# Five chained stages: shared buffers for each next stage's first loads, normalisation moved into channel attention's last pass, loops written out

## The reference

```python
x = context_xattn(x, ctx, w_q, w_k, w_v, w_o, alpha)   # 16 context rows per batch, x + alpha * delta
x = channel_xattn(x, ctx, ...)   # heads over the 256-row axis (16 heads of 64), attention between the 512 features
    # q, k, v = W @ z + Winj @ u;  x = W_o @ attention + b_o + z
    # m, var over the rows (axis 1);  (x - m) * rsqrt(var + 1e-5)
x = token_xattn(x, ctx, ...)     # layernorm, masked self attention, + x;  layernorm, cross attention, + x
    #                              then layernorm, gelu(x @ w1 + b1) @ w2 + b2, + x   (w1 512x2048, w2 2048x512)
x = recurrent(x, ...)            # layernorm, mixes, a scan over the tokens, group norm, gated feed forward
```

## Time and profile before

| | us |
|---|---|
| median of 3 runs | 3933.54 (3931.42 to 3935.23) |
| the profiled execution | 3925.65 |
| its span | 3923.7 |
| PE busy | 3475.4 (89%) |
| DVE busy | 2354.8 (60%) |
| POOL busy | 1995.9 (51%) |
| ACT busy | 1816.2 (46%) |
| PE weight loads | 2678.3 (68%) |
| mean granted clock of PE | 0.955 |

### The profile page before, as it was taken

The page is one execution under the profiler, slowest core; times in us unless marked ns, Lnnn a source line. Parts: engine busy times, 40 slices in busy tenths (PEclk is TensorE's granted clock), DMA queues, the critical chain, the costliest instruction groups (busy, mean ns, idle before and its releaser), DMA issues. The chain is left out here.

```text
span 3923.7 us, 61889 instructions
## 1 busy us (share of the span) xinstructions
PE 3475.4 (89%) x23616; PEld 2678.3 (68%) x23616; DVE 2354.8 (60%) x2915; ACT 1816.2 (46%) x4207; POOL 1995.9 (51%) x1018
## 2 busy tenths in 40 slices
PE   8979999999999999589989994999867888888876
PEld 5868778768877877277877783888745555555543
DVE  2445655565565555367778775555438677766771
ACT  1134554565465455366667664444422332333311
POOL 1135665565566556345556662455525555555562
PEclk9989999999999999799999997999989999999988
DMA  3231211111111111211021113000030000000000
GB/s 131 73 143 44 77 55 59 62 67 66 55 67 65 45 45 43 93 35 37 28 76 50 39 39 110 17 20 21 19 134 12 1 17 17 17 18 1 12 11 16
DMA packets 108138, 189.84 MB, mean 48 GB/s; under 512 B 13409, under 2 KB 32097, under 8 KB 106721
## 3 DMA queue, kind: packets, MB, share of 16 engines
q1 hardware_dynamic: 105696, 181.97, 13.5%
q10 hardware_dynamic: 2176, 4.19, 0.3%
HBM read 160.97 MB, written 25.17 MB: 47 GB/s over the span
## 5 line engine op out<-in xcount | busy, mean ns | idle before, releaser
L825 POOL TENSOR_TENSOR l_pr<-l_pr,l_inv 128x1024 f32<-128x1024 f32 x256 | 479.5, 1894 | 370.6 <-DVE l_inv L885 370.6
L734 ACT ACTIVATE l_pr<-l_ps_s,l_top 128x512 f32<-128x512 f32 x512 | 347.2, 691 | 335.2 <-DVE l_top L881 280.0
L1255 POOL TENSOR_TENSOR tok_pr<-tok_pr,tok_ma 128x1024 f32<-128x1024 f32 x128 | 305.3, 2408 | 281.5 <-DVE tok_pr L1620 281.5
L2374 POOL TENSOR_TENSOR rec_rs<-rec_sE,rec_rT 128x1024 f32<-128x1024 f32 x128 | 321.9, 2516 | 241.8 <-DVE rec_sE L2761 235.9
L820 POOL TENSOR_TENSOR l_x_lo<-l_zu,l_x_hi 128x2048 fp32r<-128x2048 f32 x63 | 288.5, 4580 | 238.6 <-ACT l_x_hi L718 238.6
L881 DVE TENSOR_REDUCE l_top<-l_ps_s 128x2 f32<-128x1024 f32 x256 | 301.3, 1219 | 11.9 <-PE l_ps_s L582 11.9
L2761 DVE TENSOR_TENSOR_SCAN rec_sE<-rec_wE,rec_ps_v 128x1024 f32<-128x1024 f32 x128 | 292.7, 2287 | 4.9
L592 PE MATMUL l_ps_t<-l_ident,l_pr 128*128 128x128 f32 x2048 | 275.4, 278 | 5.8 <-POOL l_pr L825 3.1
L592 PEld LDWEIGHTS l_ps_t<-l_ident,l_pr 128*128 128x128 f32 x2048 | 223.6, 141 | 79.2 <-issue 63.5
L1501 ACT ACTIVATE tok_pr<-tok_pr,tok_shift 128x256 f32<-128x256 f32 x512 | 253.5, 498 | 12.6 <-DVE tok_shift L1628 11.8
L739 ACT ACTIVATE l_pT<-l_ps_t 128x512 f32<-128x512 f32 x256 | 153.5, 600 | 82.6 <-PE l_ps_t L592 82.6
(11 more groups left out here) (374 smaller groups left out, 10182.6 us busy)
## 6 DMA issues: line engine op xcount, KB each, us to landing
l_zu<-x SPq DMA_DIRECT2D x64, 512.0 KB, 3.7
l_zu<-in_c SPq DMA_DIRECT2D x64, 512.0 KB, 4.6
l_w_raw<-in_L_w_qk SPq DMA_DIRECT2D x16, 512.0 KB, 6.8
tok_xs<-x SPq DMA_DIRECT2D x16, 512.0 KB, 3.9
x<-tok_xb SPq DMA_DIRECT2D x16, 512.0 KB, 2.8
l_xt<-in_xT SPq DMA_DIRECT2D x8, 512.0 KB, 6.2
l_ct<-in_cT SPq DMA_DIRECT2D x8, 512.0 KB, 7.2
l_xn<-in_x SPq DMA_DIRECT2D x8, 512.0 KB, 4.8
```

What stands on the lines that cost most here:

```text
L734: act.activation(pr[t][:, h, :], ps_s[:, t % 2, h, :], ACT.Exp, bias=top[:, t, h:h + 1], accum_out=mass[:, t, h:h + 1]).then_inc(exped, 1)
L825: pool.tensor_tensor(pr[t][:, :, :], pr[t][:, :, :], inv[:, t, :].unsqueeze(2).to_broadcast([P, 2, FEAT]), ALU.mult).then_inc(scaled, 1)
L1255: pool.tensor_tensor(tile, tile, ma[u][:, :, :].rearrange("p t k -> p (t k)").unsqueeze(1).to_broadcast([P, 2, TT * TOK]), ALU.add).then_i ...
L2374: pool.tensor_tensor(rs[j % 2][:, :, :], sE[j % 2][:, :, :], rT[s][:, :, :], ALU.mult).then_inc(rs_made, 1)
```

## The change

Three buffers belong to the whole program now (`Ahead`: two of 128x4x512, one of 128x2x512). The SP stream of a stage loads into them, near its own end, what the next stage reads first, with semaphores of the next stage that the `clear` between the two keeps: for channel attention the Q and K weights of the first pass and the first batch's rows, for the token attentions the Q and K weights and the first batch's rows, for the MLP the first two column pieces of w1 and the first batch's rows. The next stage reads them there, and its own first loads are gone; its further loads move up.

Channel attention's normalisation is done per batch during units 8 to 15 of the last pass: after a batch's last `add` VectorE sums the two row tiles (`sum_tokens`), in the next unit PE makes the mean with one matmul ahead of `mix`, VectorE centres ahead of `split_output`, ScalarE squares after `round_output`, POOL sums the two tiles of squares at the unit's end, and in the unit after that PE makes the variance with one matmul and VectorE copies it to SBUF. Logarithms and roots of batches 0 to 4 are taken in the last unit, those of 5 to 7 at the end. The stores are issued in another order.

The MLP's other twelve half pieces (128x2x512) are loaded into a ring of three buffers and rounded and split inside the first batch, two to a chunk for six chunks; b1 and b2 are loaded behind the first three halves. The `Fori` loops of token attentions, MLP and recurrent block become written-out bodies; the loop of context attention stays.

```diff
+class Ahead:
+    def __init__(self, nc, ctx):
+        self.pieces = [ctx.enter_context(nc.sbuf_tensor(f"ahead_piece{i}", [P, FT, FEAT], F32)) for i in range(2)]
+        self.rows = ctx.enter_context(nc.sbuf_tensor("ahead_rows", [P, TT, FEAT], F32))
+class AheadSignals:
+    def __init__(self, semaphores, block):
+        self.piece_loaded = [semaphores.allocate(f"{block}_piece_loaded{i}") for i in range(2)]
+        self.rows_loaded = semaphores.allocate(f"{block}_rows_loaded")
+        self.all = self.piece_loaded + [self.rows_loaded]
...
+            for src, a in enumerate((x1, c)):
+                sp.dma_start(ahead.pieces[1][:, 2 * src:2 * src + 2, :], a[0, :, :].rearrange("(t p) n -> p t n", p=P)).then_inc(following.rows_loaded, 16)
+            for part in range(2):
+                sp.dma_start(ahead.pieces[0][:, 2 * part:2 * part + 2, :].rearrange("p s n -> p (s n)"), w_after[0, :, part, :]).then_inc(
+                    following.piece_loaded[part], 16)
             for u in range(2):
...
+            return g == COUPLES and b > BATCH
+        EARLY = BATCH - 3
...
-            load_zu(1, 0)
-            load_w(0, 0)
...
+            sp.dma_start(ahead.pieces[0][:, :, :], w_after[0].rearrange("(t p) n -> p t n", p=P)).then_inc(following.piece_loaded[0], 16)
+            sp.wait_ge(x_split, of(COUPLES, UNITS - 1, 1, 0))
+            sp.dma_start(ahead.pieces[1][:, :, :], w_after[1].rearrange("(t p) n -> p t n", p=P)).then_inc(following.piece_loaded[1], 16)
...
+            store(3, 1, 2, stored)
+            store(1, 0, 2, stored)
+            store(4, 1, 3, stored)
+            sp.wait_ge(first_stored, 16)
...
+                        pe.wait_ge(*((var_kept, b - BATCH - 2) if h == 0 else (centred, b - BATCH - 1)))
                     for m in range(QT):
...
+            def means(n):
+                pe.wait_ge(mean_made, 1)
+                pe.wait_ge(presummed, n + 1)
+                if n < BATCH - 1:
+                    pe.wait_ge(turned_kept[1], of(COUPLES, BATCH + 1 + n, QT, QT - 1))
+                pe.wait_ge(centred, n)
+                pe.matmul(ps_t[1][:, :, :].rearrange("p a b -> p (a b)"), mean_of[:, :], token_sum[:, :],
+                          start=True, stop=True).then_inc(means_summed, 1)
+            def variances(n):
+                if n < 0:
+                    return
+                pe.wait_ge(sq_summed, n + 1)
+                if n == BATCH - 1:
+                    pe.wait_ge(exped, of(COUPLES, UNITS - 1, 2 * QT, 2 * QT - 1))
+                    bank = ps_s[:, 0, 0, :]
+                else:
+                    pe.wait_ge(turned_kept[0], of(COUPLES, min(BATCH + 2 + n, UNITS - 1), QT, QT - 1))
+                    pe.wait_ge(var_kept, n)
+                    bank = ps_t[0][:, :, :].rearrange("p a b -> p (a b)")
+                pe.matmul(bank, mean_of[:, :], square[:, 0, :], start=True, stop=True).then_inc(vars_summed, 1)
...
+                    variances(b - BATCH - 2)
+                    means(b - BATCH - 1)
                 mix(g, b, there)
...
-            def means(b):
-                pe.wait_ge(added, of(COUPLES, BATCH + b, CT, 1))
-                if b >= 2:
-                    pe.wait_ge(centred, b - 1)
-                for m in range(CT):
...
+            means(BATCH - 1)
+            variances(BATCH - 1)
         @block.scalar
...
+            def squares(n):
+                act.wait_ge(centred, n + 1)
+                act.wait_ge(vars_summed, n)
+                act.activation(square[:, :, :], acc[:, n, :, :], ACT.Square).then_inc(squared, 1)
...
+                if g == COUPLES and b == UNITS - 1:
+                    act.wait_ge(var_kept, EARLY)
+                    logarithms(0, EARLY)
                 round_output(g, b)
+                if normalises(g, b):
+                    squares(b - BATCH - 1)
...
+            squares(BATCH - 1)
+            act.wait_ge(var_kept, EARLY + 1)
+            logarithms(EARLY, EARLY + 1)
+            act.wait_ge(vars_summed, BATCH - 1)
+            act.activation(var[:, BATCH - 2, :], ps_t[0][:, :, :].rearrange("p a b -> p (a b)"), ACT.Ln, bias=eps[:, 0:1]).then_inc(logged, 1)
+            act.wait_ge(vars_summed, BATCH)
+            act.activation(var[:, BATCH - 1, :], ps_s[:, 0, 0, :], ACT.Ln, bias=eps[:, 0:1]).then_inc(logged, 1)
+            roots(EARLY, BATCH, 4)
         @block.gpsimd
...
+            def sum_squares(n):
+                pool.wait_ge(squared, n + 1)
+                pool.tensor_tensor(square[:, 0, :], square[:, 0, :], square[:, 1, :], ALU.add).then_inc(sq_summed, 1)
...
+                    sum_squares(b - BATCH - 1)
...
+            normalise(1, 1)
+            normalise(EARLY, 2)
...
+            def sum_tokens(n):
+                dve.wait_ge(added, of(COUPLES, BATCH + n, CT, 1))
+                dve.wait_ge(means_summed, n)
+                dve.tensor_tensor(token_sum[:, :], acc[:, n, 0, :], acc[:, n, 1, :], ALU.add).then_inc(presummed, 1)
+            def centre(n):
+                dve.wait_ge(means_summed, n + 1)
+                for m in range(CT):
+                    ins = dve.tensor_tensor(acc[:, n, m, :], acc[:, n, m, :], ps_t[1][:, :, :].rearrange("p a b -> p (a b)"), ALU.subtract)
+                ins.then_inc(centred, 1)
+            def keep_variances(n):
+                if n >= 0:
+                    dve.wait_ge(vars_summed, n + 1)
+                    dve.tensor_copy(var[:, n, :], ps_t[0][:, :, :].rearrange("p a b -> p (a b)")).then_inc(var_kept, 1)
...
+                    keep_variances(b - BATCH - 2)
+                    centre(b - BATCH - 1)
                 split_output(g, b)
                 if there(2) and makes_values(b + 2):
...
+                    sum_tokens(b - BATCH)
...
+            for n in (2, 3, 4):
+                normalise(n, 1)
+            for n in (6, 7):
+                normalise(n, 2)
...
                     batch(g, 0, Near(i * BATCH + 2, COUNT))
                     batch(g, 1, Near(i * BATCH + 3, COUNT))
...
             def before():
-                load_x(1, 0, 0)
                 for i in range(len(layers)):
                     sp.dma_start(ln_sb[i][:, :, :], layers[i].ln).then_inc(small_loaded, 16)
                     sp.dma_start(qk_sb[i][:, :, :], layers[i].qk).then_inc(small_loaded, 16)
-                load_weight("Q", 0)
                 load_rows(0)
-                load_weight("K", 0)
                 load_mask(1, 0, 0)
                 load_x(1, 1, 0)
...
+                    load_ahead()
                 if near.prev is not None:
...
+            def load_ahead():
+                sp.wait_ge(stored, at(PASSES, 2, -1, 16))
+                sp.wait_ge(biased, at(PASSES, 2, 0))
+                sp.wait_ge(normalised, at(PASSES, 2, 0))
+                sp.dma_start(ahead.rows[:, :, :], tiles(layers[-1].out, 1, 0)).then_inc(following.rows_loaded, 16)
+                for i in range(2):
+                    sp.wait_ge(w_split["VO"[i]], len(layers))
+                    sp.dma_start(ahead.pieces[i][:, :, :], weight_columns(w1_after, i)).then_inc(following.piece_loaded[i], 16)
...
+    HALVES = [(n, i, k) for n, i in (("w2", 0), ("w1", 2), ("w2", 1), ("w1", 3), ("w2", 2), ("w2", 3)) for k in range(2)]
...
-        stages = [ring[:, :, :, :].rearrange("p a b n -> p (a b n)") for ring in (pre_ring, cube_ring, xb_res)]
+        spare = sb("spare", [P, 2, FEAT])
...
+                if k >= 3:
+                    sp.wait_ge(half_split, k - 2)
...
             sp.dma_start(ln_sb[:, :, :], ln_cols).then_inc(cols_loaded, 16)
+            for k in range(3):
+                load_half(k)
             sp.dma_start(b1_sb[:, :], b1).then_inc(cols_loaded, 16)
             sp.dma_start(b2_row[:, :], b2.to_broadcast([P, FEAT])).then_inc(cols_loaded, 16)
+            for k in range(3, len(HALVES)):
+                load_half(k)
+                if k == 4:
+                    load(1)
...
-            pool.wait_ge(cols_loaded, 48)
...
+            power(0)
+            pool.wait_ge(cols_loaded, 48)
...
+                    if b == 0 and n == 7:
+                        pool.wait_ge(half_split, len(HALVES))
+                        add_bias(b)
...
+            def hidden(b, n):
+                if b == 0 and n in (0, 2):
+                    pe.wait_ge(piece_split, n // 2 + 1)
+                elif b == 0 and n in (4, 6):
+                    pe.wait_ge(half_split, halves_up_to("w1", n // 2))
...
+                if b == 0 and k % 2 == 0:
+                    pe.wait_ge(half_split, halves_up_to("w2", k // 2))
...
+            def round_half(k):
+                act.wait_ge(half_loaded[k % 3], 16 * (k // 3 + 1))
+                act.activation(half_of(k, 0), stages[k % 3], ACT.Copy).then_inc(half_hi, 1)
...
+                if b == 0 and n == 0:
+                    act.wait_ge(piece_split, 2)
...
+            for i in range(2):
+                act.wait_ge(here.piece_loaded[i], 16)
```

(36 more changed lines are left out.)

455 lines of the change are left out of this document (208 added, 247 removed).

## The result

The changed kernel takes **3898.77 us** (3896.72 to 3898.97, 4 runs) against 3932.48 (3927.5 to 3935.23, 4 runs) of the kernel before: ratio 0.9915, 95% interval 0.9897 to 0.9932, that is 26.7 to 40.5 us less. Forecast were 3902.7 and -30.8. Run again later the ratio was 0.9919 (0.9902 to 0.9935).

A forecast was written before the change was run, and what follows sets the result against it. PE was taken as the bound, busy 3475 of 3924 us, with gains in seams and loops. Terms -6.2, -5.8, -0.5, -5.6, -0.5, -0.2 and -12 sum to -30.8: 3902.7 us from the median 3933.54, range 3882 to 3918.

The forecast's parts named there:

- 1. Channel start: Start of channel attention: with inputs and weights already in place, PE starts at 216.0 instead of 222.21, -6.2 us.
- 2. Last pass: Channel attention's last pass: matmuls +10.4, token sum +10.5, end of the pass -26.7, net -5.8 us.
- rival (a): Channel's last pass: VectorE and POOL don't block each other, unit cost 3.1 instead of 10.5; total -41.6, 3892 us; chance 0.25.
- Tail: Channel's last pass, from the last add to the next block: 21.7 us against 48.4, -26.7.
- 3. Token start: Start of the token attentions: small column loads, which VectorE and ScalarE wait for, move up one place on SP, -0.5 us.
- 4. Loops: Loops written out: token back edges, where PE stands still, -5.6 us; MLP -0.5; recurrent -0.2.
- rival (d): Token loops: the 2.8 us wait isn't the branch and stays; total -25.2, 3908 us; chance 0.06.
- MLP, forecast -0.5: MLP loop written out: a step over a back edge takes 49.37 us, 49.14 without; -0.23 twice.
- Recurrent, forecast -0.2: Recurrent loop written out: two back edges gone, -0.2 us, from nothing to twice the token term's 2.8.
- 5. MLP start: MLP's first batch: PE starts 14 us earlier, half pieces are spread over six chunks, first add at 2484.5, -12 us.
- (b): Added work eats more: MLP's first batch gains only 5, channel net 0; about -17, 3916 us; chance 0.17.
- (c): Token, MLP and recurrent loops: 20 written-out bodies cost 2.8 us each, +56 against -24.7; 3965 us; chance 0.04.

## Why the prediction was right, step by step

**1. Channel start**, forecast -6.2: 12.19 to 6.15, -6.0; the last add of unit 8 in the last pass then came 6.9 earlier.

**2. Last pass.** The sequence of the unit came as reasoned. PE +10.4 and token sum +10.5 were forecast, 20.9 in sum; units 9 to 15 took 2.6, four times 3.4, 3.1 and 0.4 us more, 19.6. The sum's price was 1.6 to 1.7 instead of 1.73, and rival (a), no blocking, is refuted: the kernel with the sum moved took 1.7 us less in each of units 10 to 13. Tail: 21.8 measured, 21.7 forecast, against 48.5. The net is -7.1, forecast -5.8. Units 14 and 15 were sized too dear: 4.6 us were forecast for the two, 3.5 measured.

**3. Token start**, forecast -0.5: statistics 1.1 earlier, the first batch's add 0.4 later in the first profile. No gain is shown.

**4. Loops.** Without the loops the two waits are gone, and the batches across the back edges took 2.8 to 4.7 us less each, so rival (d), that the wait stays, is refuted. For a compare-and-branch the Trainium skill (Advanced Engine Details and Errata, Control Flow Timing) gives about 108 ns; the stall at a token back edge was 2.8 to 3.2 us in four profiles. The step's -5.6 lies inside the count of 4.4 to 6.5 only because two errors cancel: it left out what the batch across a back edge gains beyond PE's wait (45.6 or 46.9 to 42.3 in the self attention layer) and what the cross attention layer gives back, where in the loop some additions of epsilon start ahead of POOL's split. That was luck; the block itself fell by 3.6 in the first profiles. MLP, forecast -0.5: the steps are 49.27 for a mean of 49.22 over six, no gain. Recurrent, forecast -0.2: open, as said.

**5. MLP start**, forecast -12: first add -11.2. PE's start was forecast 14 us earlier and came 14.9 earlier; the first batch behind it took 63.5 us instead of 61.5. The sum in between doesn't close: six chunks at 7.2 us from 2428 give 2471 and not 2468. ScalarE's first and seventh eviction of that batch:

```profile
2410.30 0.84 ACT L2063 ACTIVATE ahead_piece<-mlp_ps_h,mlp_b 128x256 f32<-128x256 f32 x2 [6.92 <-issue]
...
2449.96 0.84 ACT L2063 ACTIVATE ahead_piece<-mlp_ps_h,mlp_b 128x256 f32<-128x256 f32 x2 [0.98 <-PE mlp_ps_h L2010]
```

They stand 39.7 us apart, in steps of 3.3 to 12.0 and not of 7.2 each; before it was 28.5. So the stated times were right and the price per chunk was not: the halves cost 11 us, and the first eviction came 22 us earlier.

**Rivals.** (b), all dearer, did not come: with the sum moved a unit took 18.84 and two matmuls, so square, POOL's sum of squares and the copies stayed hidden. (c), written-out code that costs time, is refuted: 20 bodies are fresh code now, and the MLP's steps, at 49.27, pay 0.05 each for it at most.

**The whole.** The block times give -26.9 and the medians -33.7, on either side of -30.8. By blocks the errors cancel in part: channel -14.0 for -12.0 forecast, token -3.6 for -6.1, MLP -10.8 for -12.5, recurrent +1.1 for -0.2. The mechanisms of steps 1, 2 and 5 were right; that the total came within 3 us of the medians is partly luck.

## What to carry to other kernels

Price an added VectorE instruction with two SBUF inputs by what POOL is doing at that moment: to the end of POOL's instruction, plus 0.55 us; then look for the place in the unit where POOL is just finishing and nobody waits for the result. Where two engines start within a tenth of a microsecond of each other, a change elsewhere can decide which is held; when a loop is written out, compare the step times of all batches, not the removed wait alone. Loads ahead of a seam are worth what the first consumer really waits for, 6.0, at most 1.6 and 4.9 us here, not the size of the load.

## What had not been expected of the hardware

An addition on VectorE over two elements per partition with one SBUF input was held for the whole of a POOL instruction: 0.17 us free, 2.28 to 2.40 behind the 2.4 us split, decided by a start 0.08 us later or 0.01 earlier; at equal starts to 0.01 us both came. The Trainium skill (SBUF — State Buffer, Who interferes with whom) says that issue order, not the op's shape, decides who blocks; the trace agrees. On POOL the same addition took 0.21 to 0.26.

The token stage's last two intervals took from 61 to 66 us with the same instructions: 66.1 at granted clocks of 0.91 and 0.82, 63.3 at 0.95 and 0.87, 61.4 with nothing loaded ahead at 0.95 and 0.93. That scatter is as large as several terms of the sum, so a single profile cannot size them.
